# Where ScalarE's side work stands in a slot of a state-space scan: behind the second input pass in the slots whose C product GpSimd makes

## What is computed

```python
dA = exp(clip(dt[:, :, None] * A, -5, 5))                  # per token, 512 channels, 16 states
dB = dt[:, :, None] * B[:, None, :] * u[:, :, None]
state = dA * state + dB + 1e-06                            # along the tokens of a sequence
y = sum(state * C[:, None, :], axis=-1) + D * u
x = x + (y * silu(z)) @ out_w.T
x = x + experts(layernorm(x)) + sigmoid(gate) * shared_expert(layernorm(x))
```

## Time and profile before

| | us |
|---|---|
| median of 3 runs | 2995.84 (2992.72 to 2998.47) |
| the profiled execution, its own time | 2991.94 |
| its span, first to last instruction | 2990.2 |
| first stage, from the first scan to the last | 73 to 2316 |
| busy: TensorE, VectorE, GpSimd, ScalarE | 2629.0, 2254.9, 2237.2, 2032.3 |

### The profile page before, as it was taken

How to read it: one execution, slowest core, us unless ns; L and a number is a source line. 1 busy time by engine, 2 the same in 40 slices (tenths; PEclk the granted TensorE clock), 3 DMA queues, 4 the chain that set the end, 5 groups by cost and what they waited for, 6 DMA issues and landing times. The chain is left out here.

```text
span 2990.2 us, 49244 instructions
## 1 busy us (share of the span) xinstructions
PE 2629.0 (88%) x15616; PEld 2309.2 (77%) x15616; DVE 2254.9 (75%) x4890; ACT 2032.3 (68%) x4675; POOL 2237.2 (75%) x1354
## 2 busy tenths in 40 slices
PE   7888898889888888988898888888886599999998
PEld 4777787778777777877787787777775488888887
DVE  2989889988998999899989988998999233333332
ACT  3977888888888878888887888888876133333332
POOL 2989888888888889888888988898987033333333
PEclk9889989998899988899989989998997699999999
DMA  4222222222222222222222222222221278888886
GB/s 169 82 75 75 76 76 82 76 75 81 88 89 77 77 76 85 83 75 84 78 79 75 75 78 80 75 82 78 93 72 43 75 199 200 203 200 199 200 202 155
DMA packets 138184, 309.67 MB, mean 104 GB/s; under 512 B 15040, under 2 KB 79680, under 8 KB 137792
## 3 DMA queue, kind: packets, MB, share of 16 engines
q1 hardware_dynamic: 110848, 270.03, 29.1%
q0 software_dynamic: 27072, 36.46, 6.1%
HBM read 258.42 MB, written 48.01 MB: 102 GB/s over the span
## 5 line engine op out<-in xcount | busy, mean ns | idle before, releaser
L1031 POOL TENSOR_TENSOR room<-dtu,b_all 128x1024 f32<-128x1024 f32 x512 | 1202.6, 2372 | 28.3 <-DVE dtu L1419 13.8
L810 ACT ACTIVATE bank<-room,eps_col 128x512 f32<-128x512 f32 x1024 | 693.5, 684 | 324.8 <-DVE carry L1256 222.6
L797 ACT ACTIVATE room<-room,neg_a 128x256 f32<-128x256 f32 x2048 | 868.6, 498 | 0.8 <-DVE room L1208 0.8
L603 PE MATMUL bank<-ident,room 128*128 128x128 f32 x4096 | 551.2, 291 | 245.2 <-DVE room L1251 219.5
L603 PEld LDWEIGHTS bank<-ident,room 128*128 128x128 f32 x4096 | 495.5, 150 | 298.8 <-DVE room L1251 238.1
L1020 POOL TENSOR_TENSOR room<-room,c_all 128x1024 f32<-128x1024 f32 x224 | 532.0, 2375 | 166.6 <-issue 98.7
L1242 DVE TENSOR_TENSOR_SCAN bank<-room,carry,bank 128x256 f32<-128x256 f32 x864 | 580.4, 735 | 53.1 <-ACT bank L810 52.2
L1156 POOL DMA_INDIRECT out<-room,ids x144 | 223.8, 1554 | 407.3 <-DMA out<-room,ids 191.2
L1321 DVE SCALAR_TENSOR_TENSOR hid<-hid,bank 128x256 f32<-128x256 f32 (+1 forms) x312 | 131.0, 420 | 450.6 <-ACT hid L904 450.6
L1242 DVE TENSOR_TENSOR_SCAN room<-room,carry,bank 128x256 f32<-128x256 f32 x672 | 448.1, 726 | 12.4 <-ACT bank L810 11.8
L555 PE MATMUL bank<-xnT,w_conv 128*128 128x256 f32 x3072 | 404.3, 288 | 7.0 <-ACT xnT L833 5.5
(11 more groups left out here) (150 smaller groups left out, 3152.3 us busy)
## 6 DMA issues: line engine op xcount, KB each, us to landing
b_all<-b_scratch SPq DMA_DIRECT2D x128, 512.0 KB, 4.0
c_all<-b_scratch SPq DMA_DIRECT2D x128, 512.0 KB, 5.0
room<-in_wgu SPq DMA_DIRECT2D x72, 704.0 KB, 5.9
room<-in_wd SPq DMA_DIRECT2D x72, 384.0 KB, 3.6
room<-x_by_expert SPq DMA_DIRECT2D x72, 260.0 KB, 3.0
x_in<-in_x SPq DMA_DIRECT2D x32, 256.0 KB, 5.6
x<-in_x SPq DMA_DIRECT2D x32, 256.0 KB, 2.7
out<-x SPq DMA_DIRECT2D x32, 256.0 KB, 4.2
```

What stands on the lines that cost most here:

```text
L603: last = mm(tr_bank[k][:, b * P:(b + 1) * P], v[n % VRING][:, b, k * P:(k + 1) * P], ident[:, :], is_transpose=True, start=False, stop=(n ...
L797: last = af(da[n % RING][:, b, :], dt[c.par][:, b, :], ACT.Exp, scale=neg_a[:, b, n:n + 1])
L810: af(v_slot(n, h)[:, :], v[n % VRING][:, 2 * h:2 * h + 2, :].rearrange("p b t -> p (b t)"), ACT.Identity, bias=eps_col[:, 0:1]).then_inc(v ...
L1031: nc.gpsimd.tensor_tensor(out=v[n % VRING][:, :, :], in0=dtu[:, :, :], in1=row, op=ALU.mult) \
```

## The change

In the slots whose C product GpSimd makes (0, 2, ..., 12), `keep_last` and the input pass for (s+2, 0) move ahead of all side work. In the other slots the order stays. No instruction is added or removed, and the lists of TensorE, VectorE, GpSimd and SyncE are the same as before.

```diff
                     for slot in range(NS):
-                        c, n = ahead(slot + DECAY_LEAD)
-                        if c:
-                            decays(c, n)
-                        c, n = ahead(slot + 1)
-                        if c:
-                            add_eps(c, n, 1)
-                        if post:
-                            finish(post, slot)
-                        if proj:
-                            project(proj, slot)
-                        if norm and slot == 4:
-                            norm_apply(norm)
-                        if post:
-                            for u in units_of(slot, GATE_SLOT):
-                                gate(post, u, False)
-                        if norm and slot == 14:
-                            take_normed(norm)
-                        if scan and slot in BY_POOL and scan.pos != 3:
-                            keep_last(scan, slot)
-                        c, n = ahead(slot + 2)
-                        if c:
-                            add_eps(c, n, 0)
+                        def far_decays():
+                            c, n = ahead(slot + DECAY_LEAD)
+                            if c:
+                                decays(c, n)
+
+                        def input_pass(n, h):
+                            c, n = ahead(n)
+                            if c:
+                                add_eps(c, n, h)
+
+                        def keep():
+                            if scan and scan.pos != 3:
+                                keep_last(scan, slot)
+
+                        def other():
+                            if post:
+                                finish(post, slot)
+                            if proj:
+                                project(proj, slot)
...
+                        if slot in BY_POOL:
+                            far_decays()
+                            input_pass(slot + 1, 1)
+                            keep()
+                            input_pass(slot + 2, 0)
+                            other()
+                        else:
+                            far_decays()
+                            input_pass(slot + 1, 1)
+                            other()
+                            input_pass(slot + 2, 0)
```

More of the change, by code:

```diff
@@ new lines, in input_pass @@
+                        def input_pass(n, h):
[10 more added lines that the diff above has]
+                                project(proj, slot)
+                            if norm and slot == 4:
+                                norm_apply(norm)
+                            if post:
+                                for u in units_of(slot, GATE_SLOT):
+                                    gate(post, u, False)
+                            if norm and slot == 14:
+                                take_normed(norm)
```

## The result

| kernel | median us | runs | range |
|---|---|---|---|
| before | 2995.81 | 4 | 2992.72 to 2998.47 |
| changed | 3024.41 | 4 | 3023.29 to 3025.56 |

The ratio is 1.0097 (95% interval 1.0085 to 1.0109): the change makes the kernel about 1% slower, 28.6 us. The forecast was 3025 us. The profiled execution of the changed kernel took 3025.56 us, 33.6 us more than that of before. In the changed file VectorE's and GpSimd's lines stand 16 further down: L1242 is L1258, L1321 is L1337, L1217 is L1233, L1020 is L1036.

The account below looks back on a forecast made before the run. Waits between engines were taken to bound the first stage, with no engine always busy. Losses of 43.3 us less a gain of 12.0 gave +31.3 on 2991.94, 3023.2 us; with run spread the forecast was 3025, 8-in-10 range 3006 to 3044.

Parts of the forecast that it names:

- The loss in slot 12: At slot 12, VectorE's L1321 waits for the gate's late tanh: 1.33 us a call, 1.11 us at position 0.
- Nothing behind absorbs it: In slots 11 to 15 VectorE works almost without a gap, so nothing absorbs a wait put into slot 12.
- The gain in slots 2 to 5: GpSimd starts 1.19 us earlier, xn stops waiting, uT follows the convolution: 0.52 us in 23 calls, 12.0 us.
- The loss in slot 10: keep_last and the pass for (12, 0) wait for slot 10's scans, delaying zs: 0.15 us, 0 at position 0.
- By these rows I add nothing: TensorE's clock at a chunk's start: added idling lies ahead of its last two waits for VectorE, so nothing added.
- GpSimd's lead in slots 6, 8 and 10: GpSimd's earlier start in these slots gives nothing that anyone waits for; no gain counted.
- The signs named ahead: Right: L1321 waits in all 93 places, period +1.5 us at position 3; wrong: TensorE's chunk-start clock far from 0.50.
- The rival of a lower clock: TensorE's lower clock reaches 1.3 us further into each chunk, convolution 0.65 us later: 20 us more, 3045 us; chance 0.12.

Follow-up runs that it names:

- the one with half of the wait: Kernel before, with only the carry copy ahead of the side work in slot 12, the pass for (14, 0) behind: 3007.55 us, ratio 1.0047.
- the one with cover for the tanh: The full change, with VectorE's first gate step moved behind the scans of slot 13: 2972.16 us, ratio 0.9930 to the kernel before.
- the run with the passes first: Kernel before, with only the pass for (s+2, 0) ahead of the side work in slots 2 to 10, carry copy behind: 3024.84 us, ratio 1.0101.

## Why the prediction was right, point by point

- **The loss in slot 12: right, mechanism and size.** Forecast 1.33 us a call and 1.11 at position 0; measured 1.27 to 1.31 and 1.09. Over the calls 37.5 us of the forecast 39.7; one call fewer than counted loses anything. The run with slot 12 alone, the one with half of the wait and the one with cover for the tanh all bear it out.
- **Nothing behind absorbs it: right.** Over all chunks, slots 13 to 15 together changed by 0.1 us.
- **The gain in slots 2 to 5: the mechanism right, the size off in the full change.** GpSimd's lead through the copy of state 2 is the cause: slot 2 alone brings it, the passes don't. In the full change only 4.2 us of the forecast 12 are there at slot 7. The step that failed is "Taking `uT` to start 0.04 us behind the convolution's end, it comes at 1007.24": it took that end as fixed, and at positions 0 and 1 it moved back by 0.5 and 0.4 us while the granted clock fell. Without slots 10 and 12 the whole gain was 20 us, above the forecast, but 13.0 of them are at slot 7, and the others lie in slots 7 to 11.
- **The loss in slot 10: right at positions 1 to 3, and the other sign missed at position 0.** The forecast was 3.6 us, with 0 and 7 as its ends. In the full change slots 7 to 11 are 3.4 us longer at positions 1 to 3 together. At position 0 they are 6.1 us shorter, since the wait for `zs` there ended with TensorE, and TensorE was faster there; the forecast had 0. By itself slot 10 gave +1.8 us, not told from no change.
- **"By these rows I add nothing" for the clock: right in sum and wrong in detail.** The time went with the clock twice, later at a chunk's start and earlier in slots 9 to 12: 7.8 us less gain than forecast and 6.1 us less time at position 0. That the two misses nearly cancel is luck; 3025 against 3024.4 is a better hit than the working earned. The range was wide enough for either.
- **GpSimd's lead in slots 6, 8 and 10 "gives nothing that anyone waits for": right for a lead**, since slots 4 to 8 add nothing to slot 2; but for a lag it is wrong, as the run with the passes first shows.
- **The signs named ahead.** Those of being wrong did not come: the clock in the first 3.2 us of a chunk is 0.50 to 0.53 by position (0.50 to 0.55 before), and VectorE's waits in slots 7 to 9 changed by -0.48, -0.49, -0.40 and +0.16 us. Of those of being right two came in part only. The period of a chunk grew by 1.42 us at position 3, as forecast (1.5), but elsewhere by 0.28, 1.45 and 0.91 where 0.6 to 1.0 was named. And GpSimd's 98.7 us shrank to 89.7 in that row alone: with the rows that name VectorE's scans as the releaser, its waits before its products went from 140.6 to 170.9 us.

The rival of a lower clock, 20 us more, did not come. The chunk's start had a slightly lower clock at positions 0 and 1 (0.93 for 0.95 in chunk 12), and the same kernel had a higher one further on (0.89 for 0.79). The Trainium skill, TensorE: Matmul & The Clock Gate, "What's actually happening", says that the throttled level is the default and that activity releases it. The trace agrees in that a chunk begins at 0.50 to 0.53 on average, behind a stretch in which TensorE is busy for a third of the time; it doesn't follow from that sentence that the clock should be higher in slots 9 to 12.

## What to carry to other kernels

Before a wait is moved ahead of other work in an in-order list, look at each piece of work that now stands behind it, and at who takes its result next: here one tanh of 0.36 us, for which VectorE stood ready, cost more than all the rest gained. Where several engines alternate, take a waits list as a list of places, not of prizes: 40 us of one engine's waits could be removed for nothing, while 0.46 us waits at the place where VectorE sets the pace were worth 0.53 us each. And try the parts of a reordering apart: of the seven slots changed here one was worth 20 us, one cost 37, one cost up to 8 next to the others, and the rest did nothing that can be seen.

## What the runs showed of the hardware that I had not expected

TensorE's granted clock at the same place of the program changes when another place of the loop gets longer or shorter: in slots 9 to 12 of chunk 12 it was 0.79 before and 0.89 after, though nothing was changed for TensorE, and in the kernels with slot 12 alone it moved at the chunk's start, by -0.017 to +0.023, where nothing at all was changed. In this kernel that goes with up to 0.9 us in a chunk at one position, and with either sign. From the two misses of 7.8 and 6.1 us I estimate that a sum of small terms for this kernel is uncertain by some 10 us.
